# A graph attention layer with an expert layer behind it: dense edge stage from counted edges in place of gathered source rows

## The reference, cut to what matters

```python
nodes = _layernorm(x)
h = nodes @ W + b_w                       # [2500, 512]
s_dst, s_src = h @ a[:512], h @ a[512:]
e = leaky_relu(s_dst[dst] + s_src[src] + b_a, negative_slope=0.2)
w = exp(e)
denom = segment_sum(w, dst)               # one number per node
alpha = w / denom[dst]
x = x + segment_sum(alpha[:, None] * h[src], dst)
# then, of the new x: layer norm, top 2 of 8 experts (hidden size 256, gelu), weighted sum, added to x
```

## Time and profile before

| | |
|---|---|
| median of 3 runs | 770.19 us (770.01 to 776.66) |
| the profiled execution, its span | 843.5 us |
| PE, busy | 630.6 us (75%) |
| POOL, busy | 478.4 us (57%) |
| DVE, busy | 456.8 us (54%) |
| ACT, busy | 356.8 us (42%) |

### The profile page before, as it was taken

The page is one execution under the profiler, slowest core; times in us unless marked ns, Lnnn a source line. Parts: engine busy times, 40 slices in busy tenths (PEclk is TensorE's granted clock), DMA queues, the critical chain, the costliest instruction groups (busy, mean ns, idle before and its releaser), DMA issues.

```text
span 843.5 us, 13398 instructions
## 1 busy us (share of the span) xinstructions
PE 630.6 (75%) x2874; PEld 497.9 (59%) x2875; DVE 456.8 (54%) x1139; ACT 356.8 (42%) x956; POOL 478.4 (57%) x550
## 2 busy tenths in 40 slices
PE   4997335766676757766686667774988899999992
PEld 2886224655564646655565555662645787888881
DVE  3999224564555546645555655579758433333331
ACT  3232323343443434433443434335864444545551
POOL 4461775666665666656666566501104377777773
PEclk9999677989999998798979889995998999999997
DMA  9482675656666656666666666505897277777765
GB/s 310 154 286 103 179 211 146 194 166 178 186 177 174 187 168 189 175 183 167 185 184 182 169 179 189 164 2 188 306 352 285 66 136 133 137 135 134 138 117 71
DMA packets 59260, 147.26 MB, mean 175 GB/s; under 512 B 8965, under 2 KB 18437, under 8 KB 58968
## 3 DMA queue, kind: packets, MB, share of 16 engines
q0 software_dynamic: 35216, 106.84, 50.3%
q1 hardware_dynamic: 24008, 40.01, 13.7%
HBM read 118.46 MB, written 28.35 MB: 174 GB/s over the span
## 4 chain that ended last, share of the span: by engine, by line
PE 45%; DVE 21%; issue 14%; DVEq 7%; another core or an unknown queue 6%; DMA 3%; SPq 1%; ACT 1%; POOLq 0%; POOL 0%; ACTq 0%
PE ps L686 22%; PE ps L825 8%; PE ps L839 6%; DVE acc L1171 4%; DVE S L1162 4%; DVE Wt L1150 3%; DVE junk L1096 3%; PE ps L736 2%; PE ps L815 2%; DVE rows L1089 1%; DMA x_all<-in_x_dram 1%; DVEq L1202 1%; DVEq L1171 1%; PE ps L727 1%
## 5 line engine op out<-in xcount | busy, mean ns | idle before, releaser
L686 PE MATMUL ps<-rows,S 128*128 128x257 f32 x1252 | 325.9, 423 | 156.9 <-DVE acc L1171 107.1
L508 POOL DMA_INDIRECT rows<-node_table,srcT x313 | 298.4, 953 | 178.5 <-issue 86.7
L686 PEld LDWEIGHTS ps<-rows,S 128*128 128x128 f32 x1252 | 263.1, 214 | 219.5 <-issue 160.7
L915 ACT ACTIVATE E<-sdst_w,rows 128x128 f32 x313 | 100.1, 390 | 284.0 <-DVE Wt L1150 187.7
L1171 DVE TENSOR_TENSOR acc<-acc,ps 64x514 f32 x160 | 110.1, 688 | 147.8 <-PE ps L686 68.6
L1162 DVE SCALAR_TENSOR_TENSOR S<-ps,lane,Wt 128x128 f32<-128x128 f32 x313 | 88.2, 345 | 26.3 <-issue 13.9
L915 ACT ACTIVATE ps<-sdst_w,rows 128x128 f32 x313 | 96.0, 350 | 0.0
L825 PE MATMUL ps<-W_e,xgT 128*128 x352 | 83.4, 380 | 0.0
L604 POOL DMA_INDIRECT out_dram<-y,si x44 | 70.4, 1601 | 12.1 <-issue 6.3
L825 PEld LDWEIGHTS ps<-W_e,xgT 128*128 128x128 f32 x352 | 63.4, 190 | 6.9
L645 PE MATMUL ps<-Wb,xT 128*128 128x512 f32 x240 | 56.5, 398 | 6.0 <-DVE Wb L1108 5.0
(11 more groups left out here) (202 smaller groups left out, 612.9 us busy)
## 6 DMA issues: line engine op xcount, KB each, us to landing
W_e<-in_L_ffn_W_dram SPq DMA_DIRECT2D x16, 512.0 KB, 8.9
node_table<-rows SPq DMA_DIRECT2D x20, 258.0 KB, 3.2
xf<-in_x_cols_dram SPq DMA_DIRECT2D x10, 512.0 KB, 6.1
out_dram<-acc SPq DMA_DIRECT2D x20, 256.0 KB, 2.6
xn_table<-xn SPq DMA_DIRECT2D x20, 256.0 KB, 2.4
rows<-node_table,srcT POOLq DMA_INDIRECT x313
x_all<-in_x_dram SPq DMA_DIRECT2D x19, 256.0 KB, 6.6
b_b<-in_L_ffn_b_dram SPq DMA_DIRECT2D x1, 2048.0 KB, 14.6
```

Of the source, the lines that this page charges most:

```text
L508: nc.gpsimd.indirect_dma_start(out=rows[:, g % RING, c, :], out_offset=None, in_=table, in_offset=bass.IndirectOffsetOnAxis(ap=srcT[:, GC ...
L686: m = pe.matmul(ps_agg[q][:, a, 0:HALF], S[:, w, c, :], rows[:, r, c, a * HALF:(a + 1) * HALF], start=(c == 0), stop=(c == n - 1))
L915: m = nc.scalar.activation(e[:, c, :], sdst_w[:, bass.ds(w, 1), :].rearrange("p w n -> p (w n)"), ACT.Exp, bias=bias, scale=scale)
```

## The change

The source rows are no longer gathered. h stays in SBUF as a high and a low part, and for each tile of 125 destination nodes the kernel forms a full matrix of weights to all 2500 source nodes: the weight of a pair of nodes is exp(leaky_relu(...)), times the number of edges between the two.

- **Tiles.** The 20 node tiles hold 125 nodes each (x comes padded to 128 rows a tile).
- **Node stage.** `node_rows` writes `hrow`; ACT copies its high part (`high_rows`, L919, two for each pair), POOL subtracts for the low part (`low_rows`, L504, two for each pair). DVE takes the dot products from PSUM (L1127) and multiplies them by the norm's scale (L1133). DVE also makes keys of the edges and a table that tells for each tenth of a tile (10 "halves", h) where its edges' chunks begin (`edge_keys`, `chunks_of_halves`, `chunk_table`). No store to `node_table`.
- **Counting edges.** For tile t DVE makes for 10 halves 3 pairs of one-hots each in bf16: `hot_k` (128x250, which destination and source tile, two scalars from pointers, L1238) and `hot_l` (128x128, which source within the tile, L1240). PE multiplies each pair (`count`) and gets the counts in 5 PSUM banks; `count_extras` reads the table, and closes the banks.
- **Weights.** ACT makes 20 Relu and 20 Exp of 128x125 (`weights_of`, L949, L956). DVE multiplies by the counts (`weigh`, 5 of 128x500, L1273). ACT copies the high part of the product (`high_weights`, 4 of 128x625, L968), DVE subtracts for the low part (`low_and_sums`, 4 of 128x625, L1284) and sums the weights of each destination over the 20 source tiles (L1288, reads with a step of 125 elements).
- **Products.** PE multiplies low weights with high h (20 matmuls of 512 columns, with the counts of the next tile between them) and high weights with high and low h (40). `add_x` divides by the denominator and adds x (L1294, L1296, L1299); it is for the tile before, and stands behind `weigh` and before `low_and_sums` of the next one.

```diff
+            def low_rows(u, s):
+                for j in range(2):
+                    pool.wait_ge(H_hi_ok, 2 * u + j + 1)
...
+                    nc.gpsimd.tensor_tensor(H_lo[:, 2 * u + j, :], hrow[:, s, j, :],
+                                            H_hi[:, 2 * u + j, :].bitcast(F32), ALU.subtract).then_inc(H_lo_ok, 1)
...
             for u in range(NT // 2):
                 pool.wait_ge(xT_hi, u + 1)
...
                     .then_inc(xT_lo, 1)
-                m = nc.gpsimd.memset(acc[:, 2 * u:(2 * u + 2 if u < NT // 2 - 1 else NT + 1), :, :], 0.0)
...
-            def gather(g):
-
-                if g >= RING - 1:
-                    pool.wait_ge(agg_ok, g - RING + 2)
-                for c in range(GC if g < NG - 1 else GC_LAST):
-                    nc.gpsimd.indirect_dma_start(
-                        out=rows[:, g % RING, c, :], out_offset=None, in_=table,
-                        in_offset=bass.IndirectOffsetOnAxis(ap=srcT[:, GC * g + c:GC * g + c + 1], axis=0))\
-                        .then_inc(got[g % RING], 16)
-
...
+                if u >= 1:
+                    low_rows(u - 1, (u - 1) % 2)
+            low_rows(NT // 2 - 1, 1)
...
+            def count(t, h):
+
+                pe.wait_ge(pairs_ok, HALVES * t + h + 1)
+                for c in range(BASE - h % 2):
+                    m = pe.matmul(ps_count[h // 2][:, h % 2 * HW:h % 2 * HW + HW], hot_l[:, h % SLOTS, c, :],
+                                  hot_k[:, h % SLOTS, c, :], start=(h % 2 == 0 and c == 0), stop=False)
+                m.then_inc(count_ok, 1)
...
+            def count_extras(t):
+
+                words_of(pe, [word], t)
+                more = extra_in(pe, word)
...
+                for b in range(BANKS):
+                    pe.matmul(ps_count[b][:, HW:BC], last_l[:, b, :], last_k[:, b, :], start=False, stop=True)                        .then_inc(bank_ok, 1)
...
+            def tile_products(t, s):
...
+                counts = not (peeled and t >= NT - 1)
...
+                for k in range(NT):
+                    if k % (NT // 4) == 0:
+                        pe.wait_ge(A_lo_ok, 4 * t + k // (NT // 4) + 1)
+                    m = pe.matmul(ps_agg[s][0:TN, :], A_lo[:, k, :], H_hi[:, k, :], start=(k == 0), stop=False)
+                    if k == NT - 1:
+                        m.then_inc(low_ps, 1)
+                    if k % 2 == 1 and counts:
+                        count(t + 1, k // 2)
+                if counts:
+                    count_extras(t + 1)
+                for k in range(NT):
+                    for H in (H_hi, H_lo.bitcast(F32R)):
+                        m = pe.matmul(ps_agg[s][0:TN, :], A_hi[:, s, k, :], H[:, k, :], start=False,
+                                      stop=(k == NT - 1 and H is not H_hi))
+                    if k == NT // 2:
+                        if not (peeled and t < 1):
+                            pe.wait_ge(den_ok, t)
+                        pe.wait_ge(sum_ok, t + 1)
+                        pe.matmul(ps_den[0:TN, 0:1], weight_sum[:, s, :], ones[:, :], start=True, stop=True)\
+                            .then_inc(den_ps, 1)
+                m.then_inc(agg_ok, 1)
...
-            def step(u, s, i, ahead):
...
+            def high_rows(u, s):
+                for j in range(2):
+                    act.wait_ge(row_ok, 2 * u + j + 1)
+                    nc.scalar.activation(H_hi[:, 2 * u + j, :], hrow[:, s, j, :], ACT.Copy).then_inc(H_hi_ok, 1)
...
+            def step(u, s, ahead):
 
                 if ahead > 1:
                     high_xT(u + 2, s)
                     std_of(u + 2, s)
-                if not (isinstance(u, int) and u < 1):
-                    scores(u - 1, 1 - s, i)
+                if u >= 1:
+                    high_rows(u - 1, 1 - s)
+                    scores(u - 1, 1 - s)
...
+            def weights_of(t, s, high):
...
+                dst_scores = sdst_b[:, bass.ds(t * TN, TN)]
+                for k in range(NT):
+                    m = nc.scalar.activation(weight[:, s, k, :], dst_scores, ACT.Relu, bias=ss[:, 0, k:k + 1],
+                                             scale=1.0 - SLOPE)
+                    if k % (NT // 2) == NT // 2 - 1:
+                        m.then_inc(relu_ok, 1)
+                for k in range(NT):
+                    if k % (NT // 2) == 0:
+                        act.wait_ge(relu_ok, 2 * t + k // (NT // 2) + 1)
+                    m = nc.scalar.activation(weight[:, s, k, :], weight[:, s, k, :], ACT.Exp, bias=ss[:, 1, k:k + 1])
+                    if k == NT // 2 - 1 and high is not None:
+                        high_weights(*high)
+                m.then_inc(exp_ok, 1)
+
+            def high_weights(t, s):
+
+                act.wait_ge(A_ok, BANKS * t + BANKS)
+                if not (isinstance(t, int) and t < 2):
+                    act.wait_ge(agg_ok, t - 1)
+                for q in range(4):
+                    some = slice(q * NT // 4, (q + 1) * NT // 4)
+                    nc.scalar.activation(A_hi[:, s, some, :], weight[:, s, some, :], ACT.Copy).then_inc(A_hi_ok, 1)
...
+            def tile_weights(t, s):
+                peeled = isinstance(t, int)
+                high = (t + 1, 1 - s)
+                if not (peeled and t >= NT - 2):
+                    weights_of(t + 2, s, high)
...
-            def node_rows(u, s, i):
...
-                    nc.vector.scalar_tensor_tensor(out=halves(rows[:, s, j, 0:2 * HALF])[:, :, 0:HD], in0=halves(ps_h[s][j]),
-                                                   scalar=rstd[:, s, j:j + 1], in1=halves(bw_b[:, :]),
-                                                   op0=ALU.mult, op1=ALU.add).then_inc(row_ok, 1)
-                    dve.wait_ge(row_ok, 2 * u + j + 1)
...
+                    nc.vector.scalar_tensor_tensor(out=hrow[:, s, j, :], in0=ps_h[s][j][:, :], scalar=rstd[:, s, j:j + 1],
+                                                   in1=bw_b[:, :], op0=ALU.mult, op1=ALU.add).then_inc(row_ok, 1)
...
                         nc.vector.tensor_tensor_reduce(
-                            halves(junk[:, 2 * k + j, :]), halves(rows[:, s, j, 0:2 * HALF])[:, :, 0:HD],
-                            halves(a_b[:, 1 - k, :]), 1.0, 0.0, ALU.mult, ALU.add,
-                            s_dot[:, s, k, j:j + 1]).then_inc(dot_ok, 1)
+                            junk[:, 2 * k + j, :], ps_h[s][j][:, :], a_b[:, 1 - k, :], 1.0, 0.0, ALU.mult, ALU.add,
+                            s_raw[:, s, k, j:j + 1]).then_inc(raw_ok, 1)
...
+                step(u, u % 2, 2 if u + 2 < NT // 2 else 0)
+                if u == 1:
+                    edge_keys()
+                if u == 2:
+                    chunk_thresholds()
+                    chunks_of_halves()
+                if u == 7:
+                    chunk_table()
...
+            def hot(key, low, chunk, half):
+
+                nc.vector.tensor_scalar(key, lane_k[:, :], offset[:, bass.ds(half, 1)],
+                                        keyT[:, bass.ds(chunk, 1)], ALU.add, ALU.is_equal)
...
+                return nc.vector.tensor_scalar(low, lane_l[:, :], loT[:, bass.ds(chunk, 1)], None,
+                                               ALU.is_equal)
...
+            def pairs_of(t):
+
+                words_of(dve, regs, t)
+                for h in range(HALVES):
+                    first_chunk = dve.snap(within(dve.snap(regs[h]), 0, CH - 1))
+                    if not (isinstance(t, int) and t == 0 and h < SLOTS):
+                        dve.wait_ge(count_ok, HALVES * t + h + 1 - SLOTS)
+                    for c in range(BASE - h % 2):
+                        m = hot(hot_k[:, h % SLOTS, c, :], hot_l[:, h % SLOTS, c, :], first_chunk + c, t * HALVES + h)
+                    if h % 2 == 1:
+                        m = hot(last_k[:, h // 2, :], last_l[:, h // 2, :], first_chunk + BASE - 1, t * HALVES + h)
+                    m.then_inc(pairs_ok, 1)
...
+            def weigh(t, s):
+
+                dve.wait_ge(exp_ok, t + 1)
+                for b in range(BANKS):
+                    dve.wait_ge(bank_ok, BANKS * t + b + 1)
+                    part = weight[:, s, :, b * BN:(b + 1) * BN]
+                    nc.vector.scalar_tensor_tensor(out=part, in0=part, scalar=FINITE,
+                                                   in1=ps_count[b][:, 0:BC].rearrange("p (n k) -> p k n", k=NT),
+                                                   op0=ALU.min, op1=ALU.mult).then_inc(A_ok, 1)
+
+            def low_and_sums(t, s):
+
+                if not (isinstance(t, int) and t < 1):
+                    dve.wait_ge(low_ps, t)
+                for q in range(4):
+                    some = slice(q * NT // 4, (q + 1) * NT // 4)
+                    dve.wait_ge(A_hi_ok, 4 * t + q + 1)
+                    nc.vector.tensor_tensor(A_lo[:, some, :], weight[:, s, some, :], A_hi[:, s, some, :].bitcast(F32),
+                                            ALU.subtract).then_inc(A_lo_ok, 1)
```

(29 more changed lines are left out.)

672 lines of the change are left out of this document (305 added, 367 removed).

## The result

The changed kernel takes 945.05 us (median of 4 runs, 944.37 to 946.6) against 770.1 us in the same comparison: a ratio of 1.2257, with a 95% interval of 1.2207 to 1.2306. The forecast was 936 us, 1% less, in a range of 830 to 1010. The profiled execution has a span of 943.7 us, 1.4 us from the median, so its stretches can be taken as they are.

A forecast was written before the change was run, and what follows sets the result against it. POOL's gathers were taken to bound the old kernel's edge stage (415 us), DVE the new one's. The sum: 84 ahead of the edge stage + 60 ring + 524 edge stage + 268 rest = 936 us, range 830 to 1010.

The forecast's parts named there:

- The ring in the node stage: Node stage: POOL, ACT and PE wait on each other in a circle, 8.4 us more for each of seven pairs, +60 us.
- The tile: Edge stage: DVE does everything in one row and sets a period of 25.5 us, bounds about 20 and 30.
- One-hots: Edge stage, DVE: hot_k .20 and hot_l .165 us, 30 pairs 10.9 us, assuming two pointer scalars keep the quick rate.
- Weights by counts: Edge stage, DVE: five operations of 500 elements reading PSUM with a step, 4.0 us, the middle of 2.9 and 5.15.
- The turn: Edge stage, DVE to PE and back: last count, register load from the table with branch, five matmuls; 1.5 us (.8 to 2.5).
- the older tile: Edge stage, DVE's work for the tile before: two short operations and one of 512 from PSUM, 1.2 us.
- the low parts: Edge stage, DVE: four subtractions of 625 elements, 2.9 us a tile.
- the sum: Edge stage, DVE: reduction of 2500 elements that step, 4.9 us a tile (2.7 if stepping is free, 5.5 at most).
- The tail: End of edge stage: PE's 14 us, about 7 beside DVE's last step, a cold start and the last x; 9.5 us.
- Cheap short operations: Rival, DVE's one-hots: smaller fixed part, pairs 7.9 us, period 22.5, whole 879 us; chance .18.
- PE's pace: Rival, edge stage: stepping reads free and one-hots cheap, so PE's 18 us a tile decides; 789 us, chance .08.
- Slow one-hots: Rival, DVE's one-hots: the second pointer loses the quick rate, +8.7 us a tile, 1101 us; chance .04.
- Faster than before: Rival: PE's pace in the edge stage and no waiting for the chain in the node stage; 729 us, chance .05.

The follow-up runs named there:

- the last run: Changed kernel without low parts; POOL prepares DVE's one-hot keys, DVE loads one table word, not 11, PE sums denominators: 725.7 us, .9427 of the kernel before.

## Why the prediction came out right, step by step

- **What bounded the kernel before.** POOL's gathers: the run with half of them bears it out. The 415 us were got by taking two waits (73.5 us) as the profiled execution's surplus of 73.3, which no run shows; but 770.2 less 84 and the 268 that the rest takes in the run with half the gathers is 418. Its next bound was forecast nowhere in the prediction; it is PE at 320 us of edge stage.
- **The ring in the node stage**, +60: measured 146.5 - 84 = 62.5, PE's idle time 6.7 us in the mean (7.0), the row of 24 products 7.7 (6.9). That PE's gaps are the ring's, and not those of DVE's tables, was shown by taking it away. But the ring alone is worth 37 us. The work of DVE that the prediction placed "in its idle time", and put at up to 12 us without the ring, is larger: without the ring DVE sets 7.35 us a pair, not 5.5, and 25.2 us stay. In the run without low parts, where POOL has no H_lo at all, 14.7 stay (98.7 against 84).
- **The tile**, 25.5 against 25.79, but with two errors that cancel in part. *One-hots* were priced at 10.9 and took 12.5: the step "I assume that two pointer scalars keep the quick rate" was right on the rate and left out .059 us for the pointer, 1.8 us a tile. *Weights by counts* were taken at 4.0, the middle of 2.9 and 5.15, and took 2.93: a step of 80 bytes within PSUM cost nothing, though one of 500 bytes in a reduction from SBUF cost .90 ns an element as priced. The turn (1.34 for 1.5), the older tile (1.17 for 1.2), the low parts (2.9), the sum (4.92 for 4.9) hold. So the period's hit within 1% is in part luck: +1.6 for the one-hots stands against -1.1 for the weights. PE's clock was taken at .87 and was .94; nothing hung on it.
- **What the prediction didn't see** is the load of 11 words on DVE, at the start of each tile's step. It costs nothing only because a sum of 5 us stands ahead of it; so the sum was worth 2.2 us a tile and not 4.7, as the run with the short sum showed. The earlier trace rows had .81 for a load, and the text put it into the turn on PE alone. In the changed kernel this made no difference; in the runs that shortened or moved the sum it did.
- **The tail**, 9.5 against 13.0. PE is busy for 12.07 of them. Of the last tile's 14 us of products 7 were put beside DVE's last step; only some 2 lay there, since PE ended the products of tile 18 at 664.7 us, and DVE its last sum at 666.8.
- **Rivals.** Cheap short operations: pairs would have taken 7.9; they took 12.5. PE's pace: the run with fewer products took 78 us off PE's busy time and 11 off the whole. Slow one-hots: not so, hot_k holds DVE for .25 us; at 1.0 ns an element behind .13 it would be .38. Faster than before: PE's gaps in the node stage are there, as the order said.

## What to carry to other kernels

Price the new row of the busiest engine instruction by instruction, and walk the order for a chain that closes between two engines: those two things gave the time within 1% here (with some luck in the terms), though POOL, which had been the bound, was idle afterwards. Before you shorten the last instruction of a loop's body, ask what the instruction stream does behind it: a load of registers is free behind 5 us of work and costs 1.3 to 2.8 us behind .3. To take work off an engine, move the small things that feed it (columns of keys, 20 operations of .2 us) rather than the large ones, which are slower elsewhere (a hot_l every .58 us in place of .16) or hold it up.

## What the runs showed of the hardware that was not expected

- A second pointer scalar costs VectorE .059 us for each instruction (345 to 286 ns), with the operation left as it is.
- VectorE reads PSUM with a step of 20 fp32 elements at the price of adjacent ones: 671 ns for 500, as the earlier trace rows has for 512.
- A load of 11 words into VectorE's registers takes 1.29 to 2.52 us; a load of one word took .30 on PE, and .30 to .32 on VectorE in the last run (.56 the first time). It starts up to 1.2 us before the reduction that stands ahead of it.
- A quick bf16 operation of VectorE takes 1.08 to 1.32 us in place of .34 beside fp32 additions of GpSimd of 1250 and 625 elements, and ends .08 us behind the addition; beside GpSimd's operations of 3 columns (.19 each) the 19 hot_k that meet one keep their 282 ns.
- GpSimd compares 128 bf16 elements with a pointer in .60 us alone (704 ns in the mean beside VectorE's work), VectorE in .25, one every .16.
